# Sixteen LayerNorm blocks' input loads issued from GpSimd's queue instead of SyncE's

## The reference

```python
# x: (16, 2048, 1024); H = 16 heads, d = 64
n  = layernorm(x)
xn = layernorm(n) * ln_g + ln_b
q, k, v = xn @ Wq.T + bq, xn @ Wk.T + bk, xn @ Wv.T + bv
q = softmax(q, axis=-1)          # per head, over the 64 features
k = softmax(k, axis=1)           # over the 2048 tokens
attn = einsum('bnhd,bnhl->bhdl', k, v)
y    = einsum('bnhd,bhdl->bnhl', q, attn)
x = x + (n + y)                  # called h1 here
m = layernorm(x)
h = silu(m @ wg.T / 127) * (m @ wu.T / 127)      # 3072 hidden features
x = x + h @ wd.T / 127
```

## Time and profile before

| what | us |
|---|---|
| runs without a profile, median of 2 | 4455.28 |
| those two runs | 4421.28 and 4489.27 |
| profiled execution, its own time | 4419.69 |
| its span on the slowest core (3) | 4418.0 |
| spans of the other cores | 4358.9 to 4415.5 |
| PE busy, sum over the span | 3653.8 |
| VectorE busy | 1260.9 |
| ScalarE busy | 659.0 |
| GpSimd busy | 184.8 |

### The profile page before, as it was taken

The page is one execution under the profiler, slowest core; times in us unless marked ns, Lnnn a source line. Parts: engine busy times, 40 slices in busy tenths (PEclk is TensorE's granted clock), DMA queues, the critical chain, the costliest instruction groups (busy, mean ns, idle before and its releaser), DMA issues.

```text
span 4418.0 us, 61104 instructions; the slowest of 8 cores (4358.9 to 4418.0 us)
## 1 busy us (share of the span) xinstructions
PE 3653.8 (83%) x22544; PEld 2391.1 (54%) x22544; DVE 1260.9 (29%) x2998; ACT 659.0 (15%) x1084; POOL 184.8 (4%) x348
## 2 busy tenths in 40 slices
PE   6798898748598789616898998889888988889888
PEld 4343343348243343416676766667666766667666
DVE  4312212146312311415322222223222222223222
ACT  3212212110212221200001110011101110111100
POOL 0000000100000010000000000000000000000000
PEclk9897897766799899855799999999999999999999
DMA  4111111376322322587601110111011110110010
GB/s 125 61 55 58 64 55 56 77 178 201 102 67 79 103 67 72 163 147 194 147 11 48 35 36 27 49 39 39 25 44 43 38 36 30 49 39 32 30 41 10
DMA packets 275136, 306.05 MB, mean 69 GB/s; under 512 B 158229, under 2 KB 223893, under 8 KB 272026
## 3 DMA queue, kind: packets, MB, share of 16 engines
q1 hardware_dynamic: 115994, 136.42, 10.9%
q0 software_dynamic: 34944, 136.34, 9.6%
q10 hardware_dynamic: 123904, 29.40, 3.5%
HBM read 167.86 MB, written 136.31 MB: 69 GB/s over the span
## 4 chain that ended last, share of the span: by engine, by line
PE 69%; DVE 9%; ACTq 8%; DMA 5%; issue 4%; ACT 3%; another core or an unknown queue 1%; DVEq 1%; SPq 0%; POOLq 0%; POOL 0%
PE pb L1128 25%; PE pb L636 16%; PE pb L1097 13%; PE pb L574 9%; ACTq L94 8%; DVE h_st L873 2%; PE pb L797 2%; DMA h1n_stg<-s_h 1%; DVE n_t L539 1%; DMA s_h1n_lo<-lo_tok 1%; DVE xnT_lo L547 1%; DMA kTe<-s_kT 1%; ACT xnT_hi L544 1%; PE pb L387 1%
## 5 line engine op out<-in xcount | busy, mean ns | idle before, releaser
L1128 PE MATMUL pb<-hnT_hi_b,wgT 128*128 128x256 bf16 x3072 | 842.6, 274 | 16.8 <-issue 16.8
L1128 PE MATMUL pb<-hnT_lo_b,wgT 128*128 128x256 bf16 x3072 | 842.0, 274 | 0.0
L1128 PE MATMUL pb<-hnT_hi_b,wuT 128*128 128x256 bf16 x3072 | 841.1, 274 | 0.0
L1128 PE MATMUL pb<-hnT_lo_b,wuT 128*128 128x256 bf16 x3072 | 840.6, 274 | 0.0
L1097 PE MATMUL pb<-wdT_t,hmT_hi 128*128 128x512 bf16 x1536 | 472.1, 390 | 201.5 <-DVE hmT_hi L1149 201.4
L1143 DVE SCALAR_TENSOR_TENSOR g_t<-pb,g_t 128x256 f32<-128x256 f32 x384 | 163.0, 425 | 1509.3 <-ACT g_t L1139 1483.9
L1097 PE MATMUL pb<-wdT_t,hmT_lo 128*128 128x512 bf16 x1536 | 472.7, 390 | 0.0
L1139 ACT ACTIVATE g_t<-pb 128x256 f32<-128x256 f32 x384 | 147.5, 384 | 1744.7 <-PE pb L1128 1452.7
L1128 PEld LDWEIGHTS pb<-hnT_hi_b,wgT 128*128 128x128 bf16 x3072 | 302.7, 99 | 100.1 <-issue 28.8
L1128 PEld LDWEIGHTS pb<-hnT_lo_b,wgT 128*128 128x128 bf16 x3072 | 302.5, 98 | 76.0 <-issue 4.4
L574 PE MATMUL pb<-wvT_hi,xnT_hi 128*128 128x512 bf16 x512 | 195.1, 471 | 176.0 <-DVE v_stg L604 169.6
(11 more groups left out here) (147 smaller groups left out, 3611.4 us busy)
## 6 DMA issues: line engine op xcount, KB each, us to landing
x_r<-x SPq DMA_DIRECT2D x32, 512.0 KB, 4.3
s_r<-r_r POOLq DMA_DIRECT2D x32, 512.0 KB, 4.9
s_v<-v_stg POOLq DMA_DIRECT2D x32, 512.0 KB, 3.0
s_qT<-qT_stg POOLq DMA_DIRECT2D x64, 256.0 KB, 2.8
s_kT<-kT_stg POOLq DMA_DIRECT2D x64, 256.0 KB, 2.6
kTe<-s_kT SPq DMA_DIRECT2D x16, 1024.0 KB, 5.8
v_p<-s_v SPq DMA_DIRECT2D x16, 1024.0 KB, 6.7
qT_c<-s_qT SPq DMA_DIRECT2D x32, 512.0 KB, 6.9
```

What stands on the lines that cost most here:

```text
L1128: hc=hc, bsl=bsl, st=st, sp=sp: e.matmul(pb[bnk][:, 0:256], wtt[:, d, hc * 128:(hc + 1) * 128], xt.ap()[:, bsl, d, :], start=st, stop=sp),
```

## The change

The load of `h1n_stg` in `p_stats` is issued by GpSimd's queue instead of SyncE's. Its waits stay. 32 loads of 512 KB move, two for each block.

```diff
             def f():
                 tok = b * 256 + tc * 128
                 fb = 20 * tc
-                mld = P.dma("sync", h1n_stg[:, 0, :], s_h1[tok:tok + 128, :],
+                mld = P.dma("gpsimd", h1n_stg[:, 0, :], s_h1[tok:tok + 128, :],
                             waits=[m_h1store[(tok // T, (tok % T) // 128)]]
                             + ln_stg["free"])
```

## The result

The changed kernel is slower by 1.06%: the ratio of its time to that of before is 1.0106, with a 95% interval of 1.0059 to 1.0152 (18 and 17 runs). Within 2%, as forecast, but on the other side of zero: 1.0106 times the 4419.69 us of before is 4467 us, where the forecast said 4412. The plain medians are 4519.37 and 4420.44 us; that gap is larger than the ratio because the ratio leaves out executions in which a whole die ran at a low clock. The lowest times of the two, 4430.27 and 4410.05 us, are 20 us apart.

What follows compares the result with a forecast made beforehand. The prediction took PE to bound the kernel (69% of the span), standing still for the second-half load. Its terms, -12.6 + 0.1 - 1.6 + 6 = -8 us, took 4419.69 to 4412 us, range 4382 to 4470.

Steps and rivals of the forecast that it cites:

- -12.6 us of the feed-forward stage: Step 13, 14 blocks: path from landed store to landed load falls from 5.1 to 4.2 us, -0.9 us a block.
- +0.1: Four loads of blocks 0 and 1: second +0.9 us by POOL's way, fourth -0.8 us without company, others nothing.
- -1.6: Chunk 0 of phase 3: VectorE's own waits, 1.19 us for the sums and 0.41 for the products, should go.
- The company of h_b: Second-half load, feed-forward stage: two h_b loads behind it cost 1.8 us; moving the load to POOL loses them.
- The 3 us that PE stands: Step 13: PE stands still about 3 us a block, the most a gain can reach; 14 x 3 = 42 us.
- GpSimd's issue: Second-half load: POOL adds 0.4 us from landed store to issue, and its load takes 3.7 us.
- The early loads on the transposes: Phase 3's early loads fall on the weights' transposes before block 0's first square root: +6 us, bounds 0 to 8.7.
- The start of phase 3: qT_c and r_c go out once phase 2 ends; PE gains next to nothing, VectorE's waits at chunk 0 give -1.6 us.
- B: Rival, step 13: POOL's issue costs more than the company did, from a 4.6 us load on; 4440 us, chance 0.16.
- A: Rival: company was all, POOL's load takes 2.9 us, early phase-3 loads slip between the transposes; 4393 us, chance 0.14.
- D: Rival: nothing arrives, transposes absorb the gain or bank waits hide it; within 5 us of 4420, chance inside forecast's 0.62.
- C: Rival: VectorE holds up POOL's descriptors, POOL instruction longer than 0.54 us, load 2.5 us longer; 4452 us, chance 0.08.

Runs made afterwards that it cites:

- `h1_b` apart: Kernel before, with SyncE's loads of h1_b held until the first step of their block; ratio 0.9972, 2511.2 us behind phase 2.
- the stage's own loads: Against the kernel before, only the loads of blocks 2 to 15 issued by GpSimd; ratio 1.0018, 2530.0 us behind phase 2.
- the kernel that takes the load off the path: Kernel before, with hi_tok and lo_tok given room of their own, all loads by SyncE; ratios 0.9891 and, run again, 0.9943.
- the early loads alone: Kernel before, LayerNorm loads by SyncE, phase 3's loads for chunks 0 and 1 issued ahead of them; ratio 1.0009, 2525.8 us behind phase 2.
- the two controls: The kernel before and the changed kernel, each run again without edit; ratios to the kernel before 0.9968 and 1.0064.

## Why the prediction was wrong

By the terms of its sum: the -12.6 us of the feed-forward stage came out as +12, the +0.1 and -1.6 between the first square root and phase 3 as -0.9, and the +6 for the transposes as +10. Instead of -8 us the change costs 22 behind phase 2.

**The company of h_b: wrong, and it turned the sign.** The prediction said "The company costs 4.99 - 3.2 = 1.8 us" and counted it for 14 blocks. It measured 0.1 to 0.3 us a block (from issue to statistics 3.66 and 3.46 us in the two traces of before, 3.39 with `h1_b` apart). The 4.99 us was one load, in the first block shown, on the slowest core. Of the 112 such loads in that trace, all with the same two neighbours behind them, 67 need 3.3 to 3.5 us to the statistics and 22 more than 4; in the second trace of the same kernel only 5 need more than 4. Nor does a long load need this company: with GpSimd's loads and no `h_b` behind them, more than 4 us come 0, 19 and 29 times in 112 (the changed kernel, the same again, the stage's own loads). What makes the load long on some cores in some executions stays open. The number that should have stopped me stood in my own text: 47.0 us in 14 waits is 3.4 a wait, while that block waited 4.92. I had used the mean for the length of the wait and the outlier for the gain. And the waits of the earlier trace rows were those of a core with nearly the longest waits.

**The 3 us that PE stands: one block again.** The prediction took them from 3.29 us busy in 6.30 and let a gain arrive "up to the 3 us that PE stands", 14 x 3 = 42 us in all. PE's wait at this place is 0.9 to 1.1 us a block as a mean over the cores of the two traces of before, and the kernel that takes the load off the path gained 23 us in the stage.

**GpSimd's issue: right, as a price.** Forecast was 0.4 us more from landed store to issue and a load of 3.7 us. In the changed kernel the load lands in a median of 3.5 us. The chain shows 0.50 us of issue, the mean from the store's issue to the load's went from 2.69 to 3.12 us (+0.43), and from there to the statistics it is 3.68 and 3.78 in the two traces. A load alone by SyncE takes 3.39 by the same measure, so GpSimd's costs 0.3 to 0.4 more. The whole path from `lo_tok` to the statistics was 8.18 and 7.99 us before and is 8.59 and 8.66, as means 0.54 longer. Over 14 blocks that is 7.6 us where I had -12.6. The Trainium skill, DMA: Bandwidth & Descriptors (Specifications), has about 1 us to the first byte on GpSimd's path and about 0.6 on SyncE's, an estimate of 0.4 us more. The 0.3 to 0.4 us measured from issue to statistics agree with that; the 0.43 us ahead of the issue come on top.

F grew by 12 us, though, 2280.6 against 2268.4 as means of two traces. By the traces, 9.4 of these 12 us are idle time of PE (228.8 us against 219.4, means over the cores of two traces), and 2.8 its busy time, at a mean granted clock of 0.9532 against 0.9544. So the path accounts for most of the idle time; the 1.8 us of it that are left aren't explained.

**The early loads on the transposes: right in kind, and too small.** "I take two thirds, +6 us", with 8.7 as the upper bound. A grew by 10 (74.0 against 63.9). The bound was taken from the time in which such loads occupied the engines in a stretch without the weights' transposes, 3.5 us for each MB. Beside the transposes it was 6.1, and the delay is above the bound, as the early loads alone show too (+11, with four of the five loads).

**The start of phase 3: right.** From the first square root to the first h1 it was 63.9 us before and 63.1 and 62.8 after; the sum of +0.1 and -1.6 is met within a microsecond. Its terms were not measured one by one, so they may have cancelled.

**Rivals.** B was right in sign and wrong in its condition: it asked for a POOL load of 4.6 us or more, and the load takes 3.7. The 4.6 were the old path of one block less the new issue, 5.1 - 0.5; with the means, 0.12 us from landed store to issue and 3.46 to 3.66 to the statistics, the bound is 3.0 to 3.2. A needed a POOL load of 2.9 us and transposes without a delay, and had neither. D would have been within 5 us; it was 22. C didn't happen: GpSimd's instruction for this load takes 0.54 to 0.55 us in each of 32 cases, and the load is in the mean no longer than I took it.

```profile
L94 POOL DMA_DIRECT2D h1n_stg<-s_h x32: 542/548/551, 1834.2 to 4253.7; - x32
```

(duration in ns, least, median and most.) The Trainium skill, SBUF — State Buffer (SBUF: two separate sides), warns of a VectorE that keeps GpSimd from writing descriptors; the second half's load shows nothing of it here. The first half's loads do land later, but beside `out` and `h_b`, and no run separates the two.

**What is left of 1.06%.** 22 us, 0.5%, are shown behind phase 2, twice. The remainder is in phase 1, ahead of every moved instruction, in rounds at a granted clock of 0.81 that differ between two traces of one kernel, and the unchanged kernel had three of them on a core as well. That they are drawn independently of the change is what the two controls suggest, not what they prove. Counted over the cores of each trace there are 8, 18, 8, 6, 8 and 6 of them in the six with SyncE's loads alone, and 12, 20, 12, 16, 12 and 18 in the six where GpSimd issues some or all, so a tendency isn't excluded by the traces. The ratios show none after the first: those of the five later kernels with GpSimd's loads are 0.18% above 1 in the mean, and their stretches behind phase 2 give 0.16%.

## What to carry to other kernels

A wait's mean over all its occurrences and all cores is the number to price, and a single instance on the critical chain is not: where the two differ, find out why before multiplying. Before a DMA is moved off a queue, read what stood behind it on that queue, since it will go out early; here a few loads whose results VectorE didn't take for over 100 us held up the transposes that everything waited for. And where a load is waited for because its buffer is shared with the output of the step before, 4 KB of room were worth 34 us, while changing its issuer gained nothing.

## What was not expected of the hardware

2 to 2.5 MB of plain loads beside a stream of DMA transposes that fills the engines delayed the work behind it by 10 to 11 us, where their occupation elsewhere gives 7 to 9: one transposing DMA held its issuing queue for 10.32 us and another for 7.54, against 1.4 to 4.1 for their neighbours. And the granted clock of PE stays at 0.81, neither 0.5 nor 1.0, through whole rounds of phase 1 in some executions, with a mean of 0.79 against 0.97, by pairs of neighbouring cores and at other rounds each time. Each such round costs about 23 us.
